# Projecting the context of sixteen sequences in threes, by way of DRAM, in a four-layer cross-attention kernel

## What is computed

```python
def mha(x, ctx, wq, wk, wv, wo, causal):           # per sequence
    q, k, v = x @ wq + bq, ctx @ wk + bk, ctx @ wv + bv
    return softmax(q k^T / 4 [+ mask]) v @ wo + bo   # per head
# layer 0: self attention (at 0, causal), cross attention (at 1), feed forward 256-1024-256
# layer 1: self attention (at 2, causal), cross attention (at 3), mixture of 8 experts, best 2 per token
# layer 2: self attention (at 4, with a given mask), cross attention (at 5), feed forward
# layer 3: cross attention (at 6), layer norm
```

## Time and profile before

| | |
|---|---|
| median of 3 runs | 3048.85 us (3046.82 to 3053.36) |
| the profiled execution, its own time | 3048.22 us |
| its span, first to last instruction | 3045.8 us |
| TensorE busy | 2830.4 us, 93% of the span |
| VectorE / ScalarE / GpSimd busy | 1681.8 / 1331.7 / 986.7 us |
| mean granted clock of TensorE, as a share of full speed | 0.964 |

### The profile page before, as it was taken

How to read it: one execution, slowest core, us unless ns; L and a number is a source line. 1 busy time by engine, 2 the same in 40 slices (tenths; PEclk the granted TensorE clock), 3 DMA queues, 4 the chain that set the end, 5 groups by cost and what they waited for, 6 DMA issues and landing times. The chain is left out here.

```text
span 3045.8 us, 58500 instructions
## 1 busy us (share of the span) xinstructions
PE 2830.4 (93%) x22574; PEld 2279.3 (75%) x22574; DVE 1681.8 (55%) x4086; ACT 1331.7 (44%) x2955; POOL 986.7 (32%) x1103
## 2 busy tenths in 40 slices
PE   6989999989999989975999999889999999999996
PEld 4768888768888777754888888656777777777774
DVE  4646556776755867554110010276676766767664
ACT  2535445556455455332222222245455545555442
POOL 2313224444323444322000000252344444444343
PEclk8999999999999999986999999899999999999997
DMA  9755546585664674754767766375466555666342
GB/s 141 119 72 67 63 54 89 84 114 75 75 71 59 90 98 72 190 74 135 241 225 231 224 211 220 87 111 63 53 85 76 80 79 75 82 77 78 43 50 40
DMA packets 393627, 317.68 MB, mean 104 GB/s; under 512 B 152155, under 2 KB 377307, under 8 KB 393339
## 3 DMA queue, kind: packets, MB, share of 16 engines
q1 hardware_dynamic: 370994, 276.25, 54.6%
q0 software_dynamic: 8272, 23.73, 2.8%
q10 hardware_dynamic: 14085, 13.97, 1.7%
HBM read 133.54 MB, written 36.57 MB: 56 GB/s over the span
## 5 line engine op out<-in xcount | busy, mean ns | idle before, releaser
L962 ACT ACTIVATE a_prob<-a_bank 128x512 f32<-128x512 f32 (+1 forms) x640 | 332.8, 603 | 146.5 <-PE a_bank L756 142.9
L1106 DVE TENSOR_REDUCE a_maxima<-a_bank 128x2 f32<-128x512 f32 (+3 forms) x576 | 339.2, 644 | 82.7 <-PE a_bank L736 82.0
L962 ACT ACTIVATE c_prob<-c_bank 128x512 f32<-128x512 f32 (+1 forms) x512 | 266.3, 599 | 194.7 <-PE c_bank L756 194.4
L989 ACT ACTIVATE b_group_hidden<-b_bank,b_b 128x256 f32<-128x256 f32 (+1 forms) x312 | 123.3, 452 | 387.7 <-PE b_bank L820 387.7
L1106 DVE TENSOR_REDUCE c_maxima<-c_bank 128x6 f32<-128x462 f32 (+1 forms) x448 | 260.4, 635 | 45.2 <-PE c_bank L736 43.9
L865 PE MATMUL a_bank<-a_causal_b,keep_identb 128*128 128x256 bf16 (+1 forms) x768 | 243.1, 316 | 29.9 <-DMA a_qs<-a_shift 12.9
L820 PE MATMUL b_bank<-b_group_xt,b_w 128*128 128x256 f32 (+1 forms) x1248 | 261.6, 364 | 6.3 <-DVE b_group_xt L1157 6.3
L802 PE MATMUL b_bank<-b_w,b_group_hidden 128*128 128x256 f32 x1136 | 251.7, 380 | 0.9 <-ACT b_group_hidden L989 0.9
L820 PEld LDWEIGHTS b_bank<-b_group_xt,b_w 128*128 128x128 f32 x1248 | 220.6, 192 | 33.7 <-DVE b_group_xt L1157 8.3
L802 PEld LDWEIGHTS b_bank<-b_w,b_group_hidden 128*128 128x128 f32 x1136 | 215.6, 190 | 29.7 <-ACT b_group_hidden L989 1.3
L1163 DVE TENSOR_TENSOR b_group_y<-b_bank,b_b 128x512 f32<-128x512 f32 (+1 forms) x39 | 25.1, 644 | 336.1 <-PE b_bank L802 336.1
(11 more groups left out here) (255 smaller groups left out, 6224.0 us busy)
## 6 DMA issues: line engine op xcount, KB each, us to landing
b_w<-in_L_xattn_e_w SPq DMA_DIRECT2D x78, 1024.0 KB, 7.4
a_qs<-a_parts_q SPq DMA_DIRECT2D x384, 128.0 KB
c_qs<-c_parts_q SPq DMA_DIRECT2D x288, 128.0 KB
a_ks<-a_parts_k SPq DMA_DIRECT2D x192, 128.0 KB, 5.9
c_ks<-c_parts_k SPq DMA_DIRECT2D x96, 128.0 KB, 5.5
sorted_in<-a_zeros SPq DMA_DIRECT2D x8, 1024.0 KB
b_group_x<-sorted_in SPq DMA_DIRECT2D x32, 256.0 KB, 6.8
sorted_out<-b_group_y ACTq DMA_DIRECT2D x32, 256.0 KB, 4.8
```

Of the source, the lines that this page charges most:

```text
L962: act.activation(prob[0:rows, first:first + cols], bank[0:rows, 0, 0:cols], ACT.Exp, scale=SCALE).then_inc(k.own(s), 1)
L989: ins = act.activation(hidden[:, f, 0:n], bank[:, 0, j * n:(j + 1) * n], ACT.Gelu, bias=b1[:, f:f + 1])
L1106: v.tensor_reduce(maxima[:, q:q + qn, h:h + n].rearrange("p q h -> p h q"), bank[:, 0, 0:cols].rearrange("p (j q n) -> p j q n", j=n, q=qn ...
```

## The change

Contexts are projected for three sequences at once (231 columns; the sixteenth sequence is alone). Keys: four matmuls of 231 columns. Values: two tiles of 128 and 103 rows. The parts of the keys and the values go to DRAM (`ctx_out`, six DMAs, and `val_out`, two), and each cross attention loads its own sequence's share from there (`ctx_in`, six DMAs, and `val_in`, one) into `ctx_ks` and `ctx_values`. In phase c nothing holds these projections back but their urgency. The pools `ctx_ks` and `ctx_values` have two buffers in both phases, where phase a had three. `AHEAD` has new numbers, so that all engines' rows are laid out anew in phases a and c; phase b is as it was.

```diff
+BATCH = 3
 def parts_steps(plan, b, at, role, xt, source, after=(), gives=()):
-    n = C if role == "c" else S
+    n = context_columns(b) if role == "c" else S
...
+    if role == "c":
+        for part, kind in enumerate(("high", "middle", "low")):
+            plan.step("sync", "ctx_out", b, at, part, us=1.26, lag=3.0, after=[(kind, b, at, role)], behind=[("ctx_out", b, at, part - 1)] if part else [],
+                      gives=["parts"] if part == NPART - 1 else [], landing="parts", transfers=KT, parts=parts)
+        return
...
+def context_columns(b):
+    return C * min(BATCH, B - b)
...
+def project_context(plan, b, at, behind):
+
     ctx = ("ctx_t", (b, at))
-    plan.step("sync", "ctx_load", b, at, us=0.45, lag=2.2, after=[("enter", b, PHASE_OF[at])], takes=["ctx"], landing="ctx",
-              ctx=ctx)
-    stack = parts_steps(plan, b, at, "c", ctx, ("ctx_load", b, at))
+    plan.step("sync", "ctx_load", b, at, us=0.45, lag=2.2, behind=behind, takes=["ctx"], landing="ctx", ctx=ctx)
+    parts_steps(plan, b, at, "c", ctx, ("ctx_load", b, at))
     values = value_steps(plan, b, at, "cv", ctx, ("ctx_load", b, at), after=[("proj", b, at, "c")], gives=["xt"])
+    plan.step("sync", "val_out", b, at, us=0.63 * len(context_rows(b)), lag=3.0, after=[("value", b, at)], gives=["values"], landing="values",
+              transfers=len(context_rows(b)), values=values)
+
+
+def context_steps(plan, b, at, turn):
+    stack, values = ("ctx_ks", (b, at)), ("ctx_values", (b, at))
+    plan.step("sync", "ctx_in", b, at, us=0.63 * 6, lag=2.4, after=[("ctx_out", first_of(b), at, NPART - 1)], behind=[turn],
+              takes=["stack"], landing="stack", transfers=6, stack=stack)
+    plan.step("sync", "val_in", b, at, us=0.63, lag=2.4, after=[("val_out", first_of(b), at)], behind=[("ctx_in", b, at)],
+              takes=["values"], landing="values", values=values)
     return stack, values
...
-         "c": {"enters": 2.3, "norms": 8.4, ("norms", 4): -9.6, "turns": 1.2, ("turns", 4): -0.2, "gains": 4.7,
...
+         "c": {"contexts": -3.1, ("contexts", 5): -34.6, ("contexts", 6): -36.0, "enters": -80.8,
...
             until.wait_ge(*freed(s, "ctx"))
-            sp.dma_start(tile(s, "ctx"), k.ctx_in[b]).then_inc(k.own(s), 16)
+            n = context_columns(b)
+            sp.dma_start(tile(s, "ctx")[:, :, 0:n], k.ctx_in[:, :, b * C:b * C + n]).then_inc(k.own(s), 16)
+        elif s.kind == "ctx_out":
+            n = context_columns(b)
+            until.wait_ge(*done(("high", "middle", "low")[s.part], b, at, "c"))
+            for m in range(KT):
+                sp.dma_start(k.ctx_parts[at][s.part, b:b + n // C, :].rearrange("s (p m t) -> m p s t", p=P, m=KT)[m],
+                             tile(s, "parts")[:, s.part, m, 0:n].rearrange("p (s t) -> p s t", t=C)).then_inc(k.own(s), 16)
...
+        elif s.kind == "ctx_in":
+            until.wait_ge(*done("ctx_out", first_of(b), at, NPART - 1))
+            until.wait_ge(*freed(s, "stack"))
+            for part in range(NPART):
+                for block in COPIES[False][part]:
+                    sp.dma_start(tile(s, "stack")[block * HD:(block + 1) * HD, :, :].rearrange("d h t -> d (h t)"),
+                                 k.ctx_parts[at][part, b, :].rearrange("(d n) -> d n", d=HD)).then_inc(k.own(s), 16)
...
-    pool("ctx_ks", 3 if name == "a" else 2, [STACK + NPART, H, C], BF16)
+    pool("ctx_ks", 2, [STACK + NPART, H, C], BF16)
...
         resume_steps(plan, k.loads)
+        for at in (5, 6):
+            for b in range(0, B, BATCH):
+                project_context(plan, b, at, [("enter", 0, "c")])
         for b in range(B):
             second_half(plan, b)
```

More of the change, by code:

```diff
@@ L382, in self_attention, with cross_attention @@
     return attend_steps(plan, b, at, qs, ks, values, stacked)
-def cross_attention(plan, b, at, xt, turned, context):
+def cross_attention(plan, b, at, xt, turned):
     qs = parts_steps(plan, b, at, "q", xt, turned, gives=["xt"])
-    ks, values = context
-    stacked = [("copy", b, at, (role, part)) for role in "qc" for part in range(NPART)]
+    ks, values = context_steps(plan, b, at, ("turn", b, xt[1][1]))
+    stacked = [("copy", b, at, ("q", part)) for part in range(NPART)] + [("ctx_in", b, at)]
     return attend_steps(plan, b, at, qs, ks, values, stacked)
@@ L720, in tensor_program @@
             until.wait_ge(*freed(s, "bank"))
-            for j, (first, keys) in enumerate([(0, P), (P, P)] if at in SELF else [(0, C)]):
+            for j, (first, keys) in enumerate([(0, P), (P, P)] if at in SELF else context_rows(b)):
                 for kt in range(KT):
@@ L948, in scalar_program @@
         elif s.kind == "middle":
-            parts, rest, n = tile(s, "parts"), tile(s, "rest"), C if s.part == "c" else S
+            parts, rest, n = tile(s, "parts"), tile(s, "rest"), context_columns(b) if s.part == "c" else S
             until.wait_ge(*done("rest", b, at, s.part))
@@ L964, in scalar_program @@
             bank, values = tile(s, "bank"), tile(s, "values")
-            keys, n = (P, QT) if at in SELF else (C, 1)
             until.wait_ge(*done("value_proj", b, at))
             until.wait_ge(*freed(s, "values"))
-            act.activation(values[0:keys, 0:n, 0:H, 0:HD],
-                           bank[0:keys, 0, 0:n * D].rearrange("p (t h d) -> p t h d", h=H, d=HD), ACT.Copy).then_inc(k.own(s), 1)
+            if at in CROSS:
+                until.wait_ge(*done("fill", -1, phase))
+            for rows, first, n in [(P, 0, QT)] if at in SELF else [(rows, j, 1) for j, (_, rows) in enumerate(context_rows(b))]:
+                ins = act.activation(values[0:rows, first:first + n, 0:H, 0:HD],
+                                     bank[0:rows, 0, first * D:(first + n) * D].rearrange("p (t h d) -> p t h d", h=H, d=HD), ACT.Copy)
+            ins.then_inc(k.own(s), 1)
         elif s.kind == "relu":
```

136 lines of the change are left out of this document (77 added, 59 removed).

## The result

The changed kernel takes 3126.24 us (median of 4 runs, 3122.23 to 3128.91), the kernel before took 3050.16 beside it: a ratio of 1.0248, 95% interval 1.0231 to 1.0266. That is 76 us slower. The forecast was 13 us slower; the direction was right, the size was not, and the time lies 38 us above the range (3018 to 3088).

What follows compares the result with a forecast made beforehand. PE was taken to bound the steady parts, DMA transfers the starts of phases a and c. Terms -36.8 + 2.8 + 32 + 8 + 3 + 4 = +13 gave 3061 us, 0.4% slower, range 3018 to 3088.

Steps and rivals of the forecast that it cites:

- PE work removed: Context projections in both phases: batching by three saves 36.8 us of PE work; extra turns to `pv` in phase a add 2.8.
- The wait for `shift_in`: Phase c, sequences 5 to 14: more copies ahead and less PE work to cover lengthen PE's wait, +32 us.
- the queue: Phase c: `shift_in` lands late because it stands behind queued 128 KB copies, 1.1 us each; wrong if waits stay 1 to 2 us.
- About 20 us more of phase c's span than PE's work explains: Sign expected in the new profile: phase c's span grows about 20 us beyond what PE's work accounts for.
- The middle of phase a: Middle and end of phase a: about as many late copies in both rows, 0 us, with 10 either way.
- The rival of the small rows: DRAM writes in 154-byte rows cost twice the assumed price at both starts and somewhat in the middle: 3094 or 3078; chance 0.15.
- The start of phase a: More DMAs to and from DRAM ahead of sequence 4's first `shift_in`, on full engines: +8 us, between 3 and 15.
- The start and the end of phase c: Start: more DMAs ahead of sequence 1's `shift_in`, +3 us (0 to 6); end: less PE work covering the chains, +4.
- The saved work stays saved: Rival: added copies do not hold up the small DMA, so the kernel gets faster, 3028 or 3014; chance 0.25.
- The wash: Rival: copies at 0.9 us, late ones caught up, middle of phase a 5 us better: -2, 3046; chance 0.15.
- That `ctx_parts` or `ctx_ks` would name new waits: Sign against the forecast: new waits naming `ctx_parts`, `c_ctx_ks` or `ctx_vals` would mean the trip through DRAM costs.

Runs made afterwards that it cites:

- fill18: Changed kernel with 18 idle matmuls on TensorE ahead of the attention 4 `shift_in` wait in sequences 5 to 14 of phase c: 1.0154 of the kernel before.
- late_fill_before: Kernel before, attention 4's `shift_in` one step later on SP in sequences 5 to 14 of phase c, plus 18 idle matmuls ahead of each wait: 1.0123.
- late_before: Kernel before, nothing batched, attention 4's `shift_in` one step later on SP (behind three more query copies) in sequences 5 to 14 of phase c: 1.0180.

## Why the prediction was wrong

- *PE work removed, -36.8 + 2.8.* About right (28 turns of 0.09 us are 2.5, not 2.8). A batch's keys take 1.73 us on the timeline where 256 columns take 1.89, so 1.57 from start to start for my 1.58. At full clock the trace has 27 us less work, not 34; some matmul records can be missing.
- *The wait for `shift_in`, +32.* The mechanism was right, and so was the size. The landing was to come 21.3 us after the start of the queries' projection: 2522.70 - 2501.36 = 21.3 in the sequence shown, up to 22.0 in sequences 6 to 14. The wait was to be 4.5 us: 4.3 to 5.6, 47.7 us in ten against "some 45". In the ten sequences the waits grew from 17.0 to 47.7, by 31 for my 32. That it is so close is in part luck: the 1.3 us before was read in one sequence and is 1.7 in the mean, and sequence 5, put at 0 before and 2.9 after, had 2.6 and 4.75. Only "the queue" must read "the DMA engines' backlog".
- *What I left out: the clock behind that wait.* This is the step that failed. The prediction took a wait of 4.5 us to cost 3.2 more than one of 1.3. It costs about 6: the wait, and 2.9 us of work at half clock after it. With fill18, 29 us in the changed kernel; with late_fill_before, 17 in the kernel before. "About 20 us more of phase c's span than PE's work explains" was some 69 by the trace (42 of idle time, 27 of low clock). The earlier trace rows would have raised the question: the granted clock is 1.00 in the steady part, but 0.87 and 0.78 in the stages where PE is busy 62% and 73% of the time. And two of the twelve waits of the earlier trace rows, of 3.51 and 2.33 us, already had the half clock behind them, at 1.7 us each.
- *The middle of phase a, 0 with 10 either way.* Wrong: I held the writes to DRAM to be hidden where the DMA share is 0.59, and priced them only at the two starts. Leaving five sixths of them out gives 15 us, in the middle. The rival of the small rows had 12 us at the start of phase a and 11 in phase c; it named the right transfers and in part the wrong place. With its 0.15 and the range closing at 3088 it would still not have reached 3126.
- *The start of phase a, +8.* Half seen. I counted bytes ahead of `shift_in` and SP's issues at 0.63 us; the writes are issued into a backlog and hold SP up to 5.1 us for one, which delays the input and the copies behind them (12.9 us of PE, then 11.3 when that is mended). Phase a as a whole: -8 predicted, +13 measured.
- *The start and the end of phase c, +3 and +4.* By PE's timeline from sequence 15's first `turn_shift` in phase c to the end, PE idles 6.6 us more and loses 5.0 more to the clock: 12 for 4, the clock again being what was not counted. At its start a batch's input is waited for, 6.1 us in two waits for `c_ctx_t`, which I had not foreseen (before, 1.6).
- *The rivals.* "The saved work stays saved" had the small DMA not held up; it was. The wash needed the same term smaller. That `ctx_parts` or `ctx_ks` would name new waits did not happen: the trip through DRAM is never waited for itself.

Of the missing 63 us the clock is 29 in the steady waits of phase c by run, give or take 9. The writes have 15 in phase a, give or take 7. The rest, some 19, is spread over the ends of both phases and the middle of phase a, where by the trace the loss to the low clock doubled (from 14 to 29 us between 80 and 1260 us, where the new row and the smaller pools of phase a stand beside the writes as causes); no run settles it.

## What to carry to other kernels

Price a wait of the bounding engine with what comes after it: here a wait of 1.3 us cost itself and one of 4.5 cost 7.4 in the changed kernel; in late_before, where mostly some 1.6 us are lost behind a wait, it is 6.1. Where a small DMA ends a long chain, count the bytes issued before it by anybody, and move its issue, not its queue; three copies were worth 55 us each way. And when a change lays out all engines' rows anew, run the old row with the new work, or the new row's one suspicious place alone, before you credit or blame the change itself.

## What the runs showed of the hardware

- TensorE idle for 4.3 us was followed by 6.0 us of work at 1.2 GHz. Eighteen idle matmuls in each of ten such waits kept 2.4 GHz and made the kernel 29 us faster. The length of the wait alone does not tell: before the change one of 2.33 us cost 1.7 us of work behind it, one of 2.58 nothing.
- A DMA of 24 KB issued by the scalar engine on its own queue, behind some thirteen copies of 128 KB issued by SP, landed 7.67 us later; issued by SP behind fourteen of them, 8.06. Over nine sequences both take 9.3 us in the mean to the end of PE's wait.
- One DMA from SBUF to DRAM in rows of 154 bytes held SP for 4.9 us of issuing (from 30.5 us on) when the DMA share was at 1.19, and for 0.49 in the median of 72. It is not the small rows alone: the 24 KB `shift_in` that SP began to issue at 2246.4 us held it for 5.2, with the share at 1.16 just before, for 0.77 in the median.
